# The first two up-steps of the last network moved into the second attention's block

## The chip, the cores and the metric

One core of a Trainium2 chip runs the whole program. The metric is the device time of one execution in microseconds (us). TensorE (PE) multiplies; VectorE (DVE), ScalarE (ACT) and GpSimd (Pool) work on tiles in SBUF and PSUM; SyncE (SP) issues most DMAs. Each engine works through its own instruction list in order and waits on semaphores for the others. TensorE's clock is one of two, 2.4 GHz (granted clock 1.00) or 1.2 GHz (0.50).

## The reference, cut to what matters

Two transformer layers over `x` of 2 x 1024 tokens with 256 features, all in float32. The change lies at the seam between the last two stages:

```python
x = x + _layernorm(_L0_attn_ref(_layernorm(x)))    # linear attention, 16 heads
x = x + _layernorm(_L0_ffn_ref(_layernorm(x)))     # 16 experts, top 2, and a shared network
x = x + _layernorm(_L1_attn_ref(_layernorm(x)))    # windows of 32 keys, 16 heads of 16
x = x + _layernorm(_L1_ffn_ref(_layernorm(x)))     # the last network

def _L1_ffn_ref(h_shard, w_gate_up, w_down):       # 256 -> 2 x 1024 -> 256
    gate, up = split(einsum('bsh,oh->bso', h_shard, w_gate_up))
    return einsum('bsi,hi->bsh', silu(gate) * up, w_down)
```

## The kernel before, in words

Matmuls that have to be exact are done in three passes: both operands are split into a rounded high part (ScalarE: `act_high`) and a remainder (VectorE: `dve_low`), and high x high, high x low and low x high are summed in PSUM.

**The second attention** (`window_attention`, one `nc.Block`) runs 16 jobs, `NJ = 16`: 2 batches (`NB = 8` jobs each) x 4 groups of windows x 2 groups of heads. A loop variable `i` counts the rounds in each engine's list, and every round holds pieces of several jobs, so that the job's stages overlap. TensorE in round `i`: scores of job `i` (L2841), transposes of the probabilities of job `i-2` (L2852), product with the values of job `i-3` (L2862), and, when `i-6` is odd, the output projection of job `i-6` (L2889), which waits for the eviction of the projection before. VectorE in round `i`: maximum and subtraction of job `i` (L2605, L2609), reciprocal of job `i-4` (L2634), transpose of job `i-5` (L2641), eviction of y for job `i-7` (L2650). ScalarE: the exponential of job `i` (L2740) and the copies of transposed probabilities (L2748) and raw products (L2755). Pool multiplies the products by the reciprocals (L2539) and does small work of the norms in a round's gap. Rounds 16 to 22 only finish jobs.

Scores are read from `q3`, which is filled by rearranging `q2` (`arrange`).

Around this stand two norms for the network that follows. `before` (an `AddNorm`) normalizes the attention's output y of a segment of 512 tokens, four tiles, and adds it to x: statistics on VectorE, `scale_and_shift` on Pool, `act_apply` on ScalarE, `add` (L1123). `turn` (a `TurnNorm`) normalizes the new x, transposes it on TensorE (`pe_turn`, L1157) and splits it into `xT_hi` (`act_high`) and `xT_lo` (`dve_low`). For segment 0, all of this is done in the attention's last rounds: `before.act_apply` in round 13, `before.add` and the turn's statistics in round 15, `turn.act_apply` in round 17, the transposes in round 21. In round 15, ScalarE also loads the table of the Silu.

When all engines have reached the block's end, Pool clears the semaphores of the stage, and its memset of `begun` (L1434) signals `ffn_ready`, for which every engine waits at the head of the next block.

**The last network** (`feed_forward`) handles 4 segments, each in `J = 8` steps of 128 inner features. An up-step (`pe_up`) is 12 matmuls of 128 x 512: gate and up, two halves of the features, three passes. In the first segment these are L1344, L1345 and L1348, with waits for the weights' parts. Then ScalarE does the Silu (`act_step`, L1299) and VectorE (`dve_step`) the product (L1314), its rounding (L1318) and its remainder (L1320). The down-step (`pe_down`, L1377, L1378, L1382) runs two steps behind. Up-steps alternate between two pairs of PSUM banks: up-step `n` waits until the product of step `n-2` is made. The weights come from DRAM unsplit, during the attention; they are split (L1245 and L1256 for up, L1249 and L1260 for down) in the first segment, two steps ahead of their use, steps 0 and 1 at the block's head. Also at the head, VectorE makes the statistics of `before` for segment 1, Pool scales, ScalarE applies after its first Silu (`before.act_apply(act, 1)`), and Pool adds (L1123). The turn of segment 1 gets its statistics after steps 2 and 3, is applied after step 4 and transposed on TensorE after up-step 5 and down-step 3.

## Time and profile before

| | us |
|---|---|
| median of 3 runs | 1158.51 |
| lowest and highest | 1154.85, 1162.67 |
| profiled execution | 1155.04 |
| its span | 1153.2 |
| mean granted clock of TensorE | 0.972 of full |

The times are those of an execution on the device. The profile belongs to one execution; its span runs from the first to the last instruction that it records. Starts in a timeline are counted from the span's start. A timeline's row gives start, duration, engine, line, operation, tile written and tiles read, and in square brackets how long the engine had been idle and which work released it; `x4` merges that many alike. Matmuls overlap, so the time that one takes from its queue is the distance to the next one's start.

The second attention's jobs fill the stretch up to about 1003 us, and the last network lies between about 1005 and 1147 us.

### The profile page before, as it was taken

The page shows a single profiled execution, that of the slowest core. Times are in us where ns is not written, and L with a number is a line of the kernel's source. Part 1 is how long each engine was busy: PE and PEld are TensorE (multiplying, and loading weights), DVE is VectorE, ACT ScalarE, POOL GpSimd, SP SyncE. Part 2 cuts the span into 40 slices and gives each one's busy share as a digit, 9 for nine tenths or more (in the row PEclk, how much of TensorE's full clock was granted, in tenths as well). Part 3 has the DMA queues.
Part 4 walks back from the last instruction along what each step waited for, and adds up shares of the span by engine and source line. Part 5 has one row for each costly group of instructions (what it writes and reads, how often), then busy time and mean ns, then how long its engine had stood idle before and what let it go on. Part 6 is the DMA issues. An engine that isn't in the chain of part 4 may idle for free. (4 is left out here: it accounts for less than half of the span.)

```text
span 1153.2 us, 20280 instructions
## 1 busy us (share of the span) xinstructions
PE 1114.8 (97%) x7188; PEld 960.1 (83%) x7188; DVE 743.3 (64%) x1582; ACT 525.1 (46%) x978; POOL 252.7 (22%) x290
## 2 busy tenths in 40 slices
PE   8999999999999999999999999899998889899997
PEld 7997988989989989988988888775555778788897
DVE  6665665665665665665665677755554767686556
ACT  5675344344344344344344354555552466644322
POOL 1112021021021021111111131323332556323211
PEclk9999999999999999999999999799998969999999
DMA  4001001001001001001000000853333324000001
GB/s 156 11 1 37 11 1 38 9 0 36 9 0 36 9 0 36 9 0 36 9 0 1 1 1 4 318 123 97 98 102 96 87 77 147 1 1 1 19 19 38
DMA packets 27979, 48.28 MB, mean 42 GB/s; under 512 B 4780, under 2 KB 18060, under 8 KB 26764
## 3 DMA queue, kind: packets, MB, share of 16 engines
q1 hardware_dynamic: 23980, 37.62, 10.2%
q0 software_dynamic: 3456, 9.44, 3.1%
q8 instruction: 37, 0.61, 0.2%
q10 hardware_dynamic: 480, 0.40, 0.1%
q14 instruction: 26, 0.21, 0.1%
HBM read 35.65 MB, written 9.44 MB: 39 GB/s over the span
## 5 line engine op out<-in xcount | busy, mean ns | idle before, releaser
L880 POOL TENSOR_TENSOR linear_out_row<-linear_out_row,lin_sq 128x512 f32<-128x512 f32 x62 | 89.9, 1450 | 538.3 <-ACT lin_sq L745 536.0
L43 PE MATMUL lin_bank<-keep_xT_hi,lin_w_hi 128*128 128x512 f32 x382 | 154.2, 404 | 0.0
L44 PE MATMUL lin_bank<-keep_xT_lo,lin_w_hi 128*128 128x512 f32 x382 | 151.1, 395 | 0.0
L45 PE MATMUL lin_bank<-keep_xT_hi,lin_w_lo 128*128 128x512 f32 x382 | 150.8, 395 | 0.0
L825 DVE TENSOR_TENSOR lin_st<-lin_bank,lin_mask 128x512 f32<-128x512 f32 x64 | 44.0, 691 | 160.9 <-PE lin_bank L622 160.9
L741 ACT ACTIVATE lin_o<-lin_bank 128x512 f32<-128x512 f32 x64 | 38.3, 599 | 187.7 <-PE lin_bank L653 187.7
L649 PE MATMUL lin_bank<-lin_st,lin_v 128*128 128x128 f32 x512 | 93.8, 275 | 0.0
L653 PE MATMUL lin_bank<-lin_qd,lin_state 128*128 128x128 f32 x448 | 87.2, 276 | 0.0
L45 PEld LDWEIGHTS lin_bank<-keep_xT_hi,lin_w_lo 128*128 128x128 f32 x382 | 71.8, 188 | 17.5
L44 PEld LDWEIGHTS lin_bank<-keep_xT_lo,lin_w_hi 128*128 128x128 f32 x382 | 72.0, 189 | 14.6
L43 PEld LDWEIGHTS lin_bank<-keep_xT_hi,lin_w_hi 128*128 128x128 f32 x382 | 72.0, 188 | 14.6
L649 PEld LDWEIGHTS lin_bank<-lin_st,lin_v 128*128 128x128 f32 x512 | 75.2, 192 | 0.0
L849 DVE SCALAR_TENSOR_TENSOR lin_state<-lin_state,lin_c_dec,lin_bank 128x128 f32<-128x128 f32 x192 | 65.3, 347 | 10.2 <-PE lin_bank L637 4.2
L43 PE MATMUL lin_bank<-lin_w_hi,keep_xT_hi 128*128 128x256 f32 x256 | 71.7, 280 | 0.0
L44 PE MATMUL lin_bank<-lin_w_lo,keep_xT_hi 128*128 128x256 f32 x256 | 71.5, 279 | 0.0
L45 PE MATMUL lin_bank<-lin_w_hi,keep_xT_lo 128*128 128x256 f32 x256 | 71.4, 279 | 0.0
L653 PEld LDWEIGHTS lin_bank<-lin_qd,lin_state 128*128 128x128 f32 x448 | 67.9, 192 | 0.0
L762 DVE TENSOR_TENSOR lin_g_lo<-lin_g,lin_g_hi 128x512 fp32r<-128x512 f32 x62 | 63.9, 1030 | 2.1
L710 ACT ACTIVATE lin_v<-lin_bank 128x512 f32<-128x512 f32 x64 | 38.0, 603 | 58.1 <-PE lin_bank L45 58.1
L622 PE MATMUL lin_bank<-lin_q,lin_k 128*128 128x128 f32 x512 | 63.9, 279 | 0.0
L792 DVE TENSOR_TENSOR linear_out_row<-linear_out_row,lin_bank 128x512 f32<-128x512 f32 x64 | 43.1, 685 | 30.3 <-PE lin_bank L45 30.3
L622 PEld LDWEIGHTS lin_bank<-lin_q,lin_k 128*128 128x128 f32 x512 | 61.2, 196 | 0.0
(417 smaller groups left out, 2843.2 us busy)
## 6 DMA issues: line engine op xcount, KB each, us to landing
lin_raw<-in_wp SPq DMA_DIRECT2D x7, 1024.0 KB, 4.7
experts_up_expert_up<-in_wgu SPq DMA_DIRECT2D x16, 352.0 KB, 7.3
sorted_y<-shared_loaded SPq DMA_DIRECT2D x40, 128.0 KB, 1.7
linear_out_row<-in_wdn SPq DMA_DIRECT2D x4, 704.0 KB
lin_raw_out<-in_wop SPq DMA_DIRECT2D x8, 256.0 KB, 2.6
tokens_x<-linear_out_row SPq DMA_DIRECT2D x4, 512.0 KB, 10.3
linear_out_row<-in_ffn_up SPq DMA_DIRECT2D x2, 1024.0 KB, 5.8
tail_q<-tail_qT SPq DMA_DIRECT2D x28, 64.0 KB, 2.0
```

What stands on the lines that cost most here:

```text
L43: nc.tensor.matmul(out, lh, rh, start=first, stop=False, skip_group_check=skip)
L44: nc.tensor.matmul(out, lh, rl, start=False, stop=False, skip_group_check=skip)
L45: return nc.tensor.matmul(out, ll, rh, start=False, stop=last, skip_group_check=skip)
L622: last = pe.matmul(bank[2 + a][:, cols], k[:, a, cols], q[:, a, cols], start=True, stop=True)
L649: last = pe.matmul(bank[a][:, cols], v[:, j, a, :], st[:, a, cols], start=True, stop=fresh)
L653: last = pe.matmul(bank[a][:, cols], state[:, a, j, :], qd[:, a, cols], start=False, stop=True)
L741: act.activation(o[:, a, :], bank[a][:], ACT.Copy).then_inc(o_sb, 1)
L762: dve.tensor_tensor(g_lo[:, a, :], g[:, a, :], g_hi[:, a, :].bitcast(F32), ALU.subtract).then_inc(g_sb, 1)
L792: dve.tensor_tensor(part, part, bank[4 + f][:], ALU.add).then_inc(acc_sb, 1)
L825: dve.tensor_tensor(C4(st[:, a, :]), C4(bank[2 + a][:]), mask[:, a:a + 1, :].broadcast_to([P, TPS, P]), ALU.mult).then_inc(st_sb, 1)
L849: dve.scalar_tensor_tensor(new, state[:, a, j, :], c_dec[:, a:a + 1], grown, ALU.mult, ALU.add).then_inc(state_sb, 1)
L880: pool.tensor_tensor(part, part, sq[:, a, :], ALU.add).then_inc(squares_sb, 1)
```

## The change

- **Two up-steps move.** Up-steps 0 and 1 of segment 0 are multiplied in the attention's block: up-step 0 in round 19 behind that round's output projection, after waits for the last subtraction, for the last copy of transposed probabilities and for both low parts of the turned segment; up-step 1 in round 21, behind the last output projection. The network's block begins with up-step 2. Its Silu, product and down-step of steps 0 and 1 stay there.
- **The up-weights of steps 0, 1 and 2** are rounded by ScalarE in rounds 12, 13 and 14 (`act_high_up`) and their remainder is taken by VectorE in rounds 15, 17 and 22 (`dve_low_up`). The parts of these weights lie where `q2` and `q3` were, so ScalarE waits for the last rearrangement and VectorE for the last scores. The down-weights are still split in the network's block. Splits of the steps from 3 on come behind the step three ahead of them.
- **The norms of segment 0 come sooner.** `before`'s scale and shift: Pool after job 6, not 7, with the shifts of x (`b.pool_shift_x`) after job 7, not 6; `act_apply` in round 11, not 13; `add` in round 13 and the turn's statistics in round 14, not both in round 15; the turn's scale after Pool's job 10, not 11; its apply in round 16, not 17; its transposes and high parts in round 18, its low parts in round 19, not 21.
- **Statistics of `before` for segment 1** move from the network's head into round 20.
- The PSUM banks, four semaphores, `q2` and `q3` now belong to an object (`Signals`) that both blocks share. `Fetched` holds it; the class that it was is now called `Loaded`. Norms without a turned part have four semaphores fewer.

The diff, cut to its core:

```diff
 
+class Signals:
+
+
+    NAMES = ("up_hi", "up_lo", "g_mm", "u_mm")
+
+    def __init__(self, nc, c):
+        self.made = {n: c.sem(f"ffn_{n}") for n in self.NAMES}
+        with ExitStack() as sooner:
+            self.q3 = sooner.enter_context(nc.sbuf_tensor("window_q3", [P, RR, WPAIRS, 4, WIN], F32))
+            self.q2 = sooner.enter_context(nc.sbuf_tensor("window_q2", [P, REP, WPAIRS * WIN], F32))
+        self.first = tuple(c.sb(n, [P, KT, 2 * sum(FFN)], F32R) for n in ("up_lo", "up_hi"))
+        self.bank = c.banks(8)
+
...
+
+    def __init__(self, scope, signals, others=True):
+        self.sb = scope.sb
+        self.sem = lambda name: signals.made[name] if name in signals.NAMES else scope.sem(name) if others else None
+
...
 
     def act_high(self, act, j):
 
-        w = self.widths[j]
+        self.act_high_up(act, j)
+        if not self.whole_down:
+            self.act_high_down(act, j)
+
+    def act_high_up(self, act, j):
         act.wait_ge(self.up_in, KT * DMA)
         for cols in self.columns(j):
             act.activation(self.w_hi[:, :, cols], self.raw[:, :, cols], ACT.Copy).then_inc(self.up_hi, 1)
-        if self.whole_down:
-            return
+
+    def act_high_down(self, act, j):
+        w = self.widths[j]
         act.wait_ge(self.down_in, self.J * DMA)
         act.activation(self.d_hi[0:w, j, :], self.raw_d[0:w, j, :], ACT.Copy).then_inc(self.down_hi, 1)
 
...
@@ -1405,8 +1447,10 @@
 
 
     with Scope(nc, "ffn") as c:
-        bank = c.banks(8)
-        net = Swiglu(nc, c, keep, y, bank, FFN, weights=SwigluWeights(c, FFN, fetched))
+        signals = fetched.signals
+        bank = signals.bank
+        room = Room(c, signals)
+        net = Swiglu(nc, room, keep, y, bank, FFN, weights=SwigluWeights(room, FFN, fetched, signals.first))
...
@@ -1450,16 +1494,15 @@
             def _(dve):
                 chain = Chain(dve, own)
                 dve.wait_ge(keep.ffn_ready, 1)
-                net.dve_low(dve, 0)
-                for half in range(2):
-                    before.statistics(dve, chain, 1, half)
-                net.dve_low(dve, 1)
+                net.dve_low_down(dve, 0)
                 for g in range(SEGS):
                     late = LATE if g == 0 else 0
                     for j in range(J):
-                        if g == 0 and j + 2 < J:
-                            net.dve_low(dve, j + 2)
                         net.dve_step(dve, chain, g, j)
+                        if g == 0 and j < 2:
+                            net.dve_low_down(dve, j + 1)
+                        if g == 0 and j + 3 < J:
+                            net.dve_low(dve, j + 3)
                         if 0 <= j - late < 2 and g + 1 < SEGS:
                             dve.wait_ge(before.added, g + 2)
                             turn.statistics(dve, chain, g + 1, j - late)
@@ -1486,14 +1529,15 @@
             @block.scalar
             def _(act):
                 act.wait_ge(keep.ffn_ready, 1)
-                net.act_high(act, 0)
-                net.act_high(act, 1)
+                net.act_high_down(act, 0)
                 for g in range(SEGS):
                     late = LATE if g == 0 else 0
                     for j in range(J):
-                        if g == 0 and j + 2 < J:
-                            net.act_high(act, j + 2)
                         net.act_step(act, g, j)
+                        if g == 0 and j < 2:
+                            net.act_high_down(act, j + 1)
+                        if g == 0 and j + 3 < J:
+                            net.act_high(act, j + 3)
                         if g == j == 0:
                             before.act_apply(act, 1)
                         if g + 1 < SEGS:
@@ -1523,7 +1567,8 @@
                 for g in range(SEGS):
                     pe.wait_ge(turn.low, KT * (g + 1))
                     for j in range(J):
-                        net.pe_up(pe, g, j)
+                        if g or j >= 2:
+                            net.pe_up(pe, g, j)
 
                         if j >= 2 or g:
                             n = g * J + j - 2
...
@@ -2403,13 +2449,14 @@
 
     with Scope(nc, "tail") as c:
         sb = c.sb
-        sorted_y = keep.sorted_y
-
-        q3 = sb("q3", [P, RR, WPAIRS, 4, WIN])
+        sorted_y, signals = keep.sorted_y, fetched.signals
+
+        q3, q2 = signals.q3, signals.q2
         sb("rest_of_split", [P, 256])
-        bank = c.banks(8)
+        bank = signals.bank
         net = Swiglu(nc, c, keep, y, bank, SHARED, SHARED_EARLY, keep.shared)
         net.split_before = True
+        ffn = Swiglu(nc, Room(c, signals, False), keep, y, bank, FFN, 0, SwigluWeights(Room(c, signals, False), FFN, fetched, signals.first, True), True)
...
@@ -2545,12 +2591,12 @@
                     if n == 5:
                         a.pool_shift_x(pool)
                     if n == 6:
+                        before.affine.scale_and_shift(pool, chain, 0)
+                    if n == 7:
                         b.pool_shift_x(pool)
                     if n == 8:
                         c1.add(pool)
-                    if n == 7:
-                        before.affine.scale_and_shift(pool, chain, 0)
-                    if n == 11:
+                    if n == 10:
                         turn.affine.scale_and_shift(pool, chain, 0)
 
             @block.vector
@@ -2607,9 +2653,10 @@
                         if i >= 2:
                             dve.wait_ge(prob_sb, i - 1)
                         dve.tensor_tensor(by_window(less[x]), scores, spread_w(most[x][:]), ALU.subtract).then_inc(less_sb, 1)
-                    if i == NJ - 1:
+                    if i == NJ - 3:
                         dve.wait_ge(a.shifted, a.n)
                         before.add(dve, 0)
+                    if i == NJ - 2:
                         dve.wait_ge(before.added, 1)
                         for half in range(2):
                             turn.statistics(dve, chain, 0, half)
@@ -2652,8 +2699,18 @@
                         if t < 2:
                             dve.wait_ge(y_sb, t + 1)
                             before.statistics(dve, chain, 0, t)
-                    if i == NJ + 5:
+                    if i == NJ - 1:
+                        dve.wait_ge(s_mm, NJ)
+                        ffn.dve_low_up(dve, 0)
+                    if i == NJ + 1:
+                        ffn.dve_low_up(dve, 1)
+                    if i == NJ + 3:
                         turn.dve_low(dve, 0)
+                    if i == NJ + 4:
+                        for half in range(2):
+                            before.statistics(dve, chain, 1, half)
+                    if i == NJ + 6:
+                        ffn.dve_low_up(dve, 2)
 
             @block.scalar
             def _(act):
@@ -2761,13 +2818,20 @@
                     if i == NB - 1:
                         arrange(RR + 1, 0)
                         arrange(RR + 1, 1)
-                    if i == NB + 5:
+                    if i == NB + 3:
                         before.act_apply(act, 0)
+                    if i == NB + 4:
+                        for n in range(BATCH * RR):
+                            act.wait_ge(q3_sb[n], 2)
+                        ffn.act_high_up(act, 0)
+                    if i in (NB + 5, NB + 6):
+                        ffn.act_high_up(act, i - NB - 4)
                     if i == NJ - 1:
                         act.activation(table[:], power[:, 0:1], ACT.Silu)
-                    if i == NJ + 1:
+                    if i == NJ:
                         turn.act_apply(act, 0)
-                turn.act_high(act, 0)
+                    if i == NJ + 2:
+                        turn.act_high(act, 0)
 
             @block.tensor
             def _(pe):
@@ -2873,7 +2937,7 @@
                         project_q(1, i - 4)
                     if i == 6:
                         turn_v(1)
-                    if i == NJ + 5:
+                    if i == NJ + 2:
                         turn.pe_turn(pe, 0)
                     if 6 <= i < NJ + 6 and JOBS[i - 6][1] == RR - 1:
                         n = i - 6
@@ -2889,6 +2953,13 @@
                                 last = pe.matmul(bank[5][:, a * HID:(a + 1) * HID], oP[:, b, rr, tile * P:(tile + 1) * P], wo[:, rr, :],
                                                  start=rr == 0, stop=rr == RR - 1)
                         last.then_inc(y_mm, 1)
+                    if i == NJ + 3:
+                        pe.wait_ge(less_sb, NJ)
+                        pe.wait_ge(pT_sb, NJ)
+                        pe.wait_ge(turn.low, KT)
+                        ffn.pe_up(pe, 0, 0)
+                    if i == NJ + 5:
+                        ffn.pe_up(pe, 0, 1)
```

## Rows read from the trace of the kernel before

**Rows 1.** The page, busy time, share of the span and instructions of each engine.
```profile
PE 1114.8 (97%) x7188; PEld 960.1 (83%) x7188; DVE 743.3 (64%) x1582; ACT 525.1 (46%) x978; POOL 252.7 (22%) x290
```

**Rows 2.** Windows: us, busy us and (x) instructions per engine, mean granted clock, DMA share, GB/s.
```profile
984.00:990.00 6.00, 6.00 (x45) 5.19 (x44) 4.21 (x8) 4.23 (x10) 2.15 (x3) 1.00 0.00 0
1006.00:1013.00 7.00, 7.00 (x26) 5.57 (x25) 6.11 (x19) 4.68 (x14) 1.99 (x5) 0.76 0.00 0
```

**Rows 3.** Timeline of TensorE, end of the attention: start, us, engine, line [wait <-releaser].
```profile
989.57 1.94 PE L2889 MATMUL tail_bank<-window_wo,tail_oP 128*128 128x256 f32 x8
994.26 1.08 PE L2862 MATMUL tail_bank<-tail_v,tail_pT 128*128 128x68 f32 x8 [1.02 <-ACT tail_raw_o L2755]
1001.22 1.97 PE L2889 MATMUL tail_bank<-window_wo,tail_oP 128*128 128x256 f32 x8 [0.33 <-DVE keep_y L2650]
```

**Rows 4.** Timeline of TensorE, first segment of the last network.
```profile
1005.57 0.47 PE L1344 MATMUL ffn_bank<-keep_xT_hi,ffn_w_hi 128*128 128x512 f32 x1 [2.39 <-ACT ffn_w_hi L1245]
1012.72 0.39 PE L1344 MATMUL ffn_bank<-keep_xT_hi,ffn_w_hi 128*128 128x512 f32 x1
1015.47 0.28 PE L1377 MATMUL ffn_bank<-ffn_d_hi,ffn_h_hi 128*128 128x256 f32 x1
1030.63 1.09 PE L1157 MATMUL ffn_bank<-keep_ident,window_turn_z 128*128 128x128 f32 x8 [0.83 <-ACT window_turn_z L1129]
```

**Rows 5.** Timeline of VectorE, both blocks.
```profile
985.66 0.69 DVE L2605 TENSOR_REDUCE tail_most<-tail_bank 128x16 f32<-128x512 f32 x1 [2.00 <-PE tail_bank L2841]
987.46 0.65 DVE L2650 TENSOR_TENSOR keep_y<-tail_bank,window_bo 128x512 f32<-128x512 f32 x1
989.51 1.22 DVE L1123 TENSOR_TENSOR keep_x<-keep_x,window_before_z 128x1024 f32<-128x1024 f32 x1
992.63 0.22 DVE L2634 RECIPROCAL tail_inv<-tail_raw_o 128x16 f32<-128x16 f32 x1
1003.29 0.69 DVE L2650 TENSOR_TENSOR keep_y<-tail_bank,window_bo 128x512 f32<-128x512 f32 x1 [0.89 <-PE tail_bank L2889]
1017.90 0.75 DVE L1256 TENSOR_TENSOR ffn_w_lo<-linear_out_row,ffn_w_hi 128x256 fp32r<-128x256 f32 x2
1018.91 0.68 DVE L1314 TENSOR_TENSOR ffn_h<-ffn_silu,ffn_bank 128x512 f32<-128x512 f32 x1
1020.76 0.74 DVE L1007 BATCH_NORM_STATS2 window_turn_stats<-keep_x 128x6 f32<-128x256 f32 x2
```

**Rows 6.** Timeline of Pool, both blocks.
```profile
975.57 4.53 POOL L2315 TENSOR_SCALAR keep_x<-keep_x,tail_used_shift_y 128x256 f32<-128x256 f32 x5
983.14 1.81 POOL L2293 TENSOR_TENSOR keep_x<-keep_x,tail_spare 128x768 f32<-128x768 f32 x1
1004.88 0.10 POOL L1434 MEMSET ffn_begun<- 128x1 f32 x1 [4.86 <-POOLq L2487]
1012.83 2.42 POOL L1123 TENSOR_TENSOR keep_x<-keep_x,window_before_z 128x1024 f32<-128x1024 f32 x1 [2.19 <-ACT window_before_z L1129]
```

**Rows 7.** Timeline of ScalarE, both blocks.
```profile
991.05 1.28 ACT L2767 ACT_TABLE_LOAD   x1
1005.01 0.72 ACT L1245 ACTIVATE ffn_w_hi<-linear_out_row 128x256 fp32r<-128x256 f32 x2 [3.44 <-POOL ffn_begun L1434]
1007.78 0.57 ACT L1299 ACTIVATE ffn_silu<-ffn_bank 128x512 f32<-128x512 f32 x1
1010.67 2.08 ACT L1129 ACTIVATE window_before_z<-keep_y,window_before_shift,window_before_scale 128x256 f32<-128x256 f32 x4 [2.32 <-POOL window_before_shift L1035]
```

**Rows 8.** The page, DMA issues: KB each, us from issue to landing.
```profile
linear_out_row<-in_ffn_up SPq DMA_DIRECT2D x2, 1024.0 KB, 5.8
```

**Rows 9.** Line 1256: duration in ns, least/median/most, first and last start.
```profile
L1256 DVE TENSOR_TENSOR ffn_w_lo<-linear_out_row,ffn_w_hi x16: 391/417/2437, 1005.5 to 1031.3; 128x256 fp32r<-128x256 f32 x16
```

**Rows 10.** TensorE after a long pause: timeline and window.
```profile
923.47 1.88 PE L2810 MATMUL tail_bank<-keep_ident,tail_oP 32*128 32x32 f32 x16 [4.90 <-ACT tail_oP L2680]
920.00:947.00 27.00, 19.52 (x94) 16.90 (x95) 16.56 (x44) 17.09 (x32) 15.40 (x18) 0.56 0.34 92
```

More of the change, by code:

```diff
@@ L1170, in dve_low @@
                               ALU.subtract).then_inc(self.low, 1)
-class Fetched:
+class Loaded:
     def __init__(self, c, widths, up, down):
@@ L1212, with __init__ @@
 class Swiglu:
-    def __init__(self, nc, c, keep, y, banks, widths, start=0, weights=None):
+    def __init__(self, nc, c, keep, y, banks, widths, start=0, weights=None, only_up=False):
         self.start = start
@@ L1229, in __init__ @@
         self.up_in, self.down_in, self.up_hi, self.down_hi, self.up_lo, self.down_lo = w.up_in, w.down_in, w.up_hi, w.down_hi, w.up_lo, w.down_lo
-        self.silu, self.h = c.sb("silu", [P, 2, SEG]), c.sb("h", [P, 2, SEG])
-        if not self.whole_down:
+        if not only_up:
+            self.silu, self.h = c.sb("silu", [P, 2, SEG]), c.sb("h", [P, 2, SEG])
+        if not self.whole_down and not only_up:
             self.d_lo, self.d_hi = w.d_lo, w.d_hi
@@ L1251, in dve_low, with dve_low_up @@
     def dve_low(self, dve, j):
-        w = self.widths[j]
+        self.dve_low_up(dve, j)
+        if not self.whole_down:
+            self.dve_low_down(dve, j)
+    def dve_low_up(self, dve, j):
         for i, cols in enumerate(self.columns(j)):
@@ L2245, in __init__ @@
         self.known, self.affine_ready, self.z_ready = ({k: c.sem(f"{tag}_{n}_{k}") for k in kinds} for n in ("known", "affine", "z"))
-        self.added, self.turned, self.high, self.low = (c.sem(f"{tag}_{n}") for n in ("added", "turned", "high", "low"))
+        self.added = c.sem(f"{tag}_added")
         self.z_dve = c.sem(f"{tag}_z_dve") if by_dve else None
-        self.shifted = c.sem(f"{tag}_shifted")
+        if turned:
+            self.turned, self.high, self.low, self.shifted = (c.sem(f"{tag}_{n}") for n in ("turned", "high", "low", "shifted"))
         self.z = z
```

18 lines of the change are left out of this document (11 added, 7 removed).

## The prediction

> **What bounds the kernel now.** I read the engine totals first: TensorE is busy 97% of the span, so time comes off only where it stands still or runs slowly [rows 1]. The windows then say what limits the two stages that the change joins. While scores are still being made, the tensor engine fills the window completely, 6.00 of 6 us, with VectorE at 4.21: the attention's second half is bound by matmuls [rows 2]. The start of the last network is continuous too, but its mean clock is 0.76 [rows 2]. That is 7 x (1 - 0.76) / 0.5 = 3.4 us at 1.2 GHz instead of 2.4, after which the clock is back; lost: half of it, some 1.65 us. The fall follows a pause of the engine.
>
> Where is that pause? The timeline of TensorE shows 1.02 us of waiting before the fourteenth value product, 0.33 us before the last output projection, which ends at 1001.22 + 1.97 = 1003.19 us, and 2.39 us at the block boundary [rows 3, 4]. In the network, one up-step lasts 1015.47 - 1012.72 = 2.75 us at full clock; the first two took 1012.72 - 1005.57 = 7.15 us, and 7.15 - 5.50 = 1.65 is again the clock. The next wait is 0.83 us at the turn of segment 1, which starts at 1030.63 [rows 4]. So the stretch holds 1.35 + 2.39 + 1.65 + 0.83 = 6.2 us that are not work at full speed. The change can have that at the most.
>
> **The attention's tail.** Two up-steps move in front of the block's end: 2 x 2.75 = 5.50 us of matmuls. They don't lie beside other work of TensorE, they lengthen its queue there by as much. What can be won are its waits, so I laid out the four queues with the durations of the rows, job by job.
>
> Job 13: VectorE now has 2.00 us of waiting ahead of job 14's maximum [rows 5]. The add of segment 0 (1.22 us) moves into it, ends near 983.6, and the wait is still about 1.4 us long: free, if nothing holds the add up. For it ScalarE's norm comes two jobs sooner, and Pool's scale and shift goes ahead of the 4.53 us of shifts that started at 975.57 [rows 6]; both have the room, and the shifts end 2 us later, at 982.6.
>
> Job 14: add and statistics took 992.63 - 989.51 = 3.12 us, 1.25 of it for the add, so the statistics take 1.87 [rows 5]. They stand ahead of the transpose and of the eviction of y. Scores 14 still come at 985.66, so the difference ends at 987.1, the statistics at 988.9, transpose and reciprocal at 989.3, the eviction at 990.0 instead of 987.46 + 0.65 = 988.1. The ninth output projection, which started at 989.57 [rows 3], waits for that eviction: 0.5 us. The subtraction of job 15 ends at 991.4, not 989.6. ScalarE's last exponential, its copies and the table load of 1.28 us [rows 7] follow, 1.8 us later than before, less what ScalarE waited: value product 13 waits some 0.5 us for its predecessor's copy, and product 14 0.7 us. Then the transposes come right after product 15, near 998.7, and projection 13. The new wait of TensorE, for the low part of the turned segment, comes at 1001.5; ScalarE's and VectorE's copies (1.08 and 1.29 us, one after the other) end near 1002.2: 0.7 us. Behind that wait stands the last projection, and for that the last eviction. Sum of waits: 0.5 + 0.5 + 0.7 + 0.7 = 2.4 against 1.35. The second up-step therefore ends at 1003.19 + 5.50 + 1.05 = 1009.7.
>
> The weight splits cost VectorE 0.75 us each [rows 5], in jobs 15, 17 and 22, and ScalarE 0.72 us each [rows 7] at jobs 12 to 14, where it waits for VectorE. The last split and the last eviction, 1.4 us together, are covered by the second up-step's 2.75. Statistics of segment 1, 1.9 us, fall between evictions, covered by the first. The weights are long in SBUF: issued before 964, they land in about 6 us [rows 8]. The loads are the same and keep their place on SP's queue; no DMA is added. Fewer semaphores and the other place of two buffers: nothing.
>
> **The boundary.** Before, the block ended with VectorE's eviction, at 1003.29 + 0.69 = 1003.98, and Pool's memset that starts the network came 0.90 us later [rows 5, 6]. Now TensorE is last, so the memset is at 1010.6. But the third up-step needs the product of the first in the same PSUM bank. Released by the memset come 0.13 us to ScalarE, 0.31 for one rounding of down-weights (from the start of one activation to the next), 0.57 for the Silu, 0.04, VectorE's product 0.69 and 0.08. Up-step 3 starts at 1009.7 + 0.90 + 1.82 = 1012.4 where it was at 1012.72 [rows 4, 7]: -0.3 us. The pause of TensorE is 2.7 us, longer than the 2.39 that it replaces. **The clock** thus falls again: between 0 (if it does not) and 1.65 us, and I take 1.65, since the nearest pause is shorter and paid it.
>
> **The first segment.** From up-step 3 to the turn took 1029.80 - 1012.72 = 17.08 us; now TensorE is there at 1012.4 + 17.08 + 1.65 = 1031.2. Is z there? VectorE begins its first product at 1011.7. A step is 1020.76 - 1018.91 = 1.85, a split of up and down 1.01, its down part about 0.3, half of the statistics 0.94 [rows 5]. It waits for the second Silu, which stands behind ScalarE's 2.08 us norm [rows 7] (end of Silu: 1015.4), and its cast behind Pool's 2.42 us add, until 1017.3. Then 1.07 for cast and rest, 0.33 + 1.01 + 1.85 + 1.01 + 0.94 + 1.85 + 1.01 + 0.94: the statistics are done at 1027.4. Pool 2.1 to 2.8 and ScalarE 2.08 follow: 1031.6 to 1032.3, middle 1032.0 against 1030.63. The stall shrinks but stays, and the sum is +1.4 us.
>
> One step in this rests on row and rule. The split that met Pool's add took 2437 ns instead of a median 417 [rows 6, 9]. The Trainium skill (SBUF — State Buffer, Who interferes with whom) says that a VectorE instruction with two SBUF inputs and a GpSimd instruction that reads SBUF use a shared port, and that the second waits for the whole of the first; the trace agrees with the 2437 ns.
>
> **The sum.** The profiled execution took 1155.04 us around its span of 1153.2, so 1156.4 by this; it lies 3.5 below the median of the three runs. From that median, 1158.51, I get 1159.9.
>
> **Rivals.** *The tail is filled.* My waits rest on chains of four engines laid out by hand; my layout of the old tail was 0.5 us off. If the two up-steps swallow all but 0.3 us of waits, the second ends at 1007.6, and everything behind it starts 2.1 us sooner; VectorE's chain then lets the turn start at 1029.9 in the middle, and if its backlog is gone as well and the clock stays, at 1027.4. That is -0.7 to -3.2, middle -2: 1156.5. For it: removing 3.1 us from VectorE between the last difference and the last value products. Against it: statistics in job 14 delay the same difference. Chance 0.22.
>
> *Slower by the port.* The moved add has two SBUF inputs. At its old place, 989.51, Pool was idle; at 982.4 Pool is at its shifts, then at the product of job 8 and at a 1.8 us add. If VectorE loses, it waits until 985.0, 2.6 us, and 1.4 of that is covered: the point from which it decides. The first two weight splits can meet Pool's 0.62 us products as well. Price: 1.2 + 2 x 0.6 = 2.4 on top of 1.4, +3.8: 1162.3. The 2437 ns [rows 9] speak for a price of up to 2.0 for one collision, the slack of VectorE against it. Chance 0.14. By the rule of the Trainium skill named above, the loser is whichever issues second, so it would go this way only if Pool is first.
>
> *The clock stays down.* After a pause of 4.90 us, and with waits between its matmuls behind it, TensorE had a mean clock of 0.56 over the 27 us from 920 to 947 [rows 10]: 27 x 0.44 / 0.5 = 24 us at 1.2 GHz. If the new pause of 2.7 us and a late product did that here, 24 us at half speed would cost 12 in place of 1.65: +11.8, so 1170.3. Against it: it needs waits inside the first steps, and VectorE has its products ready there. Chance 0.02.
>
> *The change does nothing at all*, because matmuls are neither added nor removed: this is what my forecast nearly says.
>
> **Chances.** Forecast (0 to +2.7) 0.62. A measurement of this kernel can tell about 1% (11.6 us) from no change; only the last rival and an unforeseen mishap pass it: slower 0.02, faster 0.01, same 0.97. The runs shown reach from 3.7 below to 4.2 above their median. So the range goes from 1158.5 - 2 - 2.5 = 1154 to 1158.5 + 2.7 + 3.8 = 1165, which holds the forecast, most of the filled tail and of the port.
>
> **What would show it.** Right: two up-steps among the last projections, and a wait of some 0.7 us ahead of the first; a pause near 2.7 us at the boundary that ends with VectorE's product; again some 3.4 us at 0.5 behind it; the turn's start between 1031.5 and 1032.5. Wrong: a boundary pause below 2 us, a clock that holds, an add of over 1.3 us in job 13, or a turn without a wait.

## The result, and the profile after

The changed kernel took 1163.15 us in the median of 20 executions (1158.46 to 1166.64); the kernel before took 1158.42 (1154.85 to 1162.67) beside it. The ratio is 1.0037, 95% interval 1.0025 to 1.0049. By the ratio that is 4.3 us more (2.9 to 5.7), under 1%; forecast were 1.4. The median lies inside the forecast's range of 1154 to 1165, but that range was wide because single executions scatter: the loss itself lies above the 0 to 2.7 us that the prediction gave for it.

The engine totals of the changed kernel, to be held against [rows 1]:

```profile
span 1161.0 us, 20285 instructions
...
PE 1118.2 (96%) x7188; PEld 961.4 (83%) x7188; DVE 743.4 (64%) x1582; ACT 525.7 (45%) x978; POOL 254.4 (22%) x290
```

TensorE's busy time grew too, which says little, since a matmul at 1.2 GHz is busy for longer. The timeline says more. Here is TensorE in the attention's tail, the counterpart of [rows 3] (start and duration in us, engine, line, tiles; in brackets the idle time ahead and its releaser). The first row is the start of job 15's scores, from which I count below:

```profile
992.37 0.48 PE L2905 MATMUL window_bank<-linear_out_row,window_q 64*128 64x128 f32 x2
...
995.49 0.67 PE L2953 MATMUL window_bank<-window_wo,tail_oP 128*128 128x256 f32 x2 [0.36 <-DVE keep_y L2697]
...
998.25 0.52 PE L2926 MATMUL window_bank<-tail_v,tail_pT 128*128 128x68 f32 x3 [0.36 <-ACT tail_raw_o L2812]
...
1000.54 0.52 PE L2926 MATMUL window_bank<-tail_v,tail_pT 128*128 128x68 f32 x3 [0.77 <-ACT tail_raw_o L2812]
...
1005.06 0.60 PE L2953 MATMUL window_bank<-window_wo,tail_oP 128*128 128x256 f32 x2
...
1007.00 0.47 PE L1386 MATMUL window_bank<-keep_xT_hi,window_up_hi 128*128 128x512 f32 x1
...
1009.84 0.59 PE L2953 MATMUL window_bank<-window_wo,tail_oP 128*128 128x256 f32 x2
```

Three waits, 0.36 + 0.36 + 0.77 us. The first up-step (1007.00) begins right behind projection 13, without a wait. Now the boundary and the first segment, [rows 4] of before. The second row is the fourth up-step, the third row the turn of segment 1:

```profile
1017.35 0.76 PE L1386 MATMUL window_bank<-keep_xT_hi,window_up_hi 128*128 128x512 f32 x1 [2.86 <-ACT window_up_hi L1281]
...
1023.88 0.50 PE L1386 MATMUL window_bank<-keep_xT_hi,window_up_hi 128*128 128x512 f32 x1 [0.63 <-DVE ffn_h L1356]
...
1038.67 0.55 PE L1157 MATMUL window_bank<-keep_ident,window_turn_z 128*128 128x128 f32 x3 [1.94 <-ACT window_turn_z L1129]
```

Two stretches of the same engine, answering to [rows 2] (length, busy us and count, mean granted clock, DMA share, GB/s): behind the pause the clock is low again.

```profile
1007.00:1014.00 7.00, 7.00 (x31) 1.00 0.00 0
1018.00:1022.00 4.00, 4.00 (x15) 0.69 0.00 0
```

The turn came 1030.63 - 986.98 = 43.65 us after job 15's scores before [rows 4], and comes 1038.67 - 992.37 = 46.30 after them now: **2.65 us of the loss lie here.** What made it late is on VectorE. These are its rows, answering to [rows 5]: first product, the remainders of the down-weights of steps 1 and 3 (counted from 0), second product, end of the turn's statistics:

```profile
1016.41 0.69 DVE L1356 TENSOR_TENSOR ffn_h<-ffn_silu,window_bank 128x512 f32<-128x512 f32 x1
...
1018.21 0.42 DVE L1302 TENSOR_TENSOR ffn_d_lo<-linear_out_row,ffn_d_hi 128x256 fp32r<-128x256 f32 x1
...
1021.29 1.94 DVE L1302 TENSOR_TENSOR ffn_d_lo<-linear_out_row,ffn_d_hi 128x256 fp32r<-128x256 f32 x1 [1.99 <-ACT ffn_d_hi L1286]
...
1023.15 0.67 DVE L1356 TENSOR_TENSOR ffn_h<-ffn_silu,window_bank 128x512 f32<-128x512 f32 x1
...
1033.69 0.25 DVE L1012 BATCH_NORM_AGGREGATE window_turn_mean_var<-window_turn_stats 128x2 f32<-128x6 f32 x2
```

And ScalarE's and Pool's for the same time, answering to [rows 6, 7]: ScalarE's roundings of the down-weights of steps 1 and 3, the first part of its norm, the second Silu, the rounding of step 2; then Pool's add:

```profile
1016.28 0.41 ACT L1286 ACTIVATE ffn_d_hi<-linear_out_row 128x256 fp32r<-128x256 f32 x1
...
1017.20 0.40 ACT L1286 ACTIVATE ffn_d_hi<-linear_out_row 128x256 fp32r<-128x256 f32 x1
...
1018.38 0.60 ACT L1129 ACTIVATE window_before_z<-keep_y,window_before_shift,window_before_scale 128x256 f32<-128x256 f32 x1 [0.78 <-POOL window_before_shift L1035]
...
1020.37 0.57 ACT L1341 ACTIVATE ffn_silu<-window_bank 128x512 f32<-128x512 f32 x1
...
1020.85 0.41 ACT L1286 ACTIVATE ffn_d_hi<-linear_out_row 128x256 fp32r<-128x256 f32 x1
...
1020.54 2.40 POOL L1123 TENSOR_TENSOR keep_x<-keep_x,window_before_z 128x1024 f32<-128x1024 f32 x1 [2.19 <-ACT window_before_z L1129]
```

VectorE stood still for 1.99 us ahead of 1021.29, and the profile names ScalarE's `ffn_d_hi` as the releaser. The remainder that waited is that of **step 3**, and ScalarE had rounded the down-weights of step 3 long before, at 1017.20. But all these roundings raise one counter, `down_hi`, and VectorE waits for step 3 with "at least 4". ScalarE's new order is 0, 1, 3, then the norm (2.08 us), the second Silu, and only then 2, at 1020.85. The counter reaches 4 with the rounding of step 2: the wait is for the wrong data. In addition the delayed instruction now falls into Pool's add of 2.40 us and takes 1.94 us in place of the 0.42 of its like (1018.21). So the second product starts at 1023.15.

The profiled span is 1161.0 - 1153.2 = 7.8 us longer, and not all of it is the change's. From the first up-step of the shared network to job 0's scores: 42.2 us before, 47.5 after. But the kernel before, profiled a second time, had 46.5 there, and the changed one 42.9. So this part varies by 4.3 and 4.6 us between two executions of one program.

### The profile page after: what moved, and what is told of

Its sections match the earlier page's. It is cut to its first block and busy times, and to the rows that moved or that the text cites. A ratio compares the mean times of both kernels' runs of the same rounds, so it can differ in the third digit from the quotient of the medians.

```text
span 1161.0 us, 20285 instructions
## 1 busy us (share of the span) xinstructions
PE 1118.2 (96%) x7188; PEld 961.4 (83%) x7188; DVE 743.4 (64%) x1582; ACT 525.7 (45%) x978; POOL 254.4 (22%) x290
```

## The experiments

Twelve runs, each timed in five rounds; the ratio is to the kernel before, timed beside it. "Job 7 to 11" and "job 15 to turn" are distances on TensorE between starts of scores and, for the last, the start of the turn's transposes for segment 1; "turn to turn" goes on from there to the transposes for segment 2. "Low" is the time at 1.2 GHz in that distance, from its mean granted clock, and good to about 0.4 us.

| kernel | ratio, 95% interval | job 7 to 11 (low) | job 15 to turn (low) | turn to turn (low) |
|---|---|---|---|---|
| before | | 15.44 (3.4) | 43.65 (3.5) | 26.32 (0) |
| before_again | 0.9998, 0.9980 to 1.0017 | 15.44 (3.4) | 43.64 (3.5) | 26.32 (0) |
| placed | 1.0002, 0.9987 to 1.0016 | 15.30 (0) | 43.60 (0) | 26.33 (0) |
| norms | 1.0012, 0.9998 to 1.0027 | 15.44 (3.4) | 44.87 (3.6) | 26.08 (0) |
| changed | 1.0037, 1.0025 to 1.0049 | 17.07 (6.8) | 46.30 (3.7) | 26.08 (0) |
| again | 1.0030, 1.0018 to 1.0041 | 18.33 (7.0) | 46.23 (0) | 27.67 (3.4) |
| third | 1.0020, 1.0003 to 1.0038 | 18.33 (7.0) | 46.26 (0) | 27.68 (3.4) |
| in_order | 1.0013, 1.0002 to 1.0024 | 18.34 (7.0) | 44.88 (0) | 26.33 (0) |
| in_order_again | 1.0006, 0.9989 to 1.0022 | 18.32 (7.0) | 44.89 (0) | 26.32 (0) |
| one_step | 1.0008, 0.9998 to 1.0018 | 15.30 (0) | 44.95 (0) | 26.32 (0) |
| both | 1.0011, 0.9997 to 1.0024 | 15.29 (0) | 43.60 (0) | 27.91 (3.4) |
| early_two | 0.9999, 0.9985 to 1.0013 | 19.95 (10.4) | 43.61 (3.5) | 26.27 (0) |
| early_one | 0.9997, 0.9984 to 1.0010 | 15.30 (0) | 43.50 (3.5) | 26.27 (0) |
| early_one_again | 0.9983, 0.9968 to 0.9997 | 15.30 (0) | 41.79 (0) | 26.27 (0) |

From job 11 to job 15 it is 13.95 to 13.97 us in all of them, and from the second turn to the end of the span 96.3.

### Is it the orders, or where things lie? (placed, again)

placed has the shared object, its buffers and semaphores, but every engine's order of before; in outline, against the kernel before:

```diff
 class Signals: ...            # as in the change
-    bank = c.banks(8)
+    bank = signals.bank       # and q2, q3, up_lo, up_hi from it
```

> The shared object, the other places of two buffers and the shared PSUM banks alone; every list of instructions in the order of before. Theory 1 (the loss is made at the seam between the blocks, by the order of the work): as before, ratio 1.000, and the stretch from job 12's scores to the turn of segment 1 is 53.1 us long as before. Rival (the placement itself costs what the seam does not explain, some 2 us of the 4.7): ratio 1.002, and the head of the attention's block, from the first up-step of the shared network to the first transposes of values, is longer than the 40.4 us of before.

again is the changed kernel once more.

> The changed kernel once more, for a second profile. Its first profile has 5.4 us more than before ahead of job 12's scores, 5.9 of them in one gap near 895, in which VectorE and ScalarE both stand still, and 2.7 us more at the seam. Theory 1: the gap is chance and does not come again at this place, the 2.7 us do; ratio 1.002 to 1.005. Rival (the gap belongs to the change): it is there again.

placed costs nothing: 1.0002, and 43.60. Again lost 3.5 us (2.1 to 4.7), and 46.23 between job 15 and the turn. The loss comes from the orders. The column up to the turn shows something else: in placed and in again the clock **did not fall** behind the boundary, and the distance to the turn stayed the same as with the fall. Here is again:

```profile
1013.99 0.47 PE L1386 MATMUL window_bank<-keep_xT_hi,window_up_hi 128*128 128x512 f32 x1 [2.90 <-ACT window_up_hi L1281]
...
1020.45 0.50 PE L1386 MATMUL window_bank<-keep_xT_hi,window_up_hi 128*128 128x512 f32 x1 [2.02 <-DVE ffn_h L1356]
...
1035.22 0.55 PE L1157 MATMUL window_bank<-keep_ident,window_turn_z 128*128 128x128 f32 x3 [1.93 <-ACT window_turn_z L1129]
```

Clock full, so TensorE is ready for the fourth up-step 1.4 us sooner, and the fourth waits for VectorE's product 2.02 us where it waited 0.63. The low clock in this place is hidden by VectorE's chain. In placed the fourth up-step waits 1.27 us in the same way, and the distance is that of before.

But in again the clock fell a little later, behind the turn's wait of 1.93 us. Again's TensorE from 1036 to 1040 us, and its next turn:

```profile
1036.00:1040.00 4.00, 4.00 (x13) 0.57 0.00 0
...
1062.89 1.03 PE L1157 MATMUL window_bank<-keep_ident,window_turn_z 128*128 128x128 f32 x8
```

There nothing hides it: from turn to turn it takes 27.67 us, in the first profile of the same program, where the clock held, 26.08. third and both show the same fall at the same place (27.68 and 27.91), the eleven other profiles none. The changed kernel paid for no low clock between job 15 and the second turn in one profile, and 1.6 us in two; the kernel before in neither of its two.

### The counter (in_order)

The changed kernel, with this:

```diff
-                        if g == 0 and j < 2:
-                            net.dve_low_down(dve, j + 1)
+                        if g == 0 and j == 0:
+                            net.dve_low_down(dve, 1)
+                            net.dve_low_down(dve, 2)
```

and the same for ScalarE's `act_high_down`, so that the counter rises in the order of the waits.

> The changed kernel with the down-weights of steps 1 and 2 both rounded and subtracted ahead of those of step 3, so that the counter of rounded down-weights rises in the order in which VectorE waits for it. Theory 1 (the remainder of down-weights 3 waits for the rounding of down-weights 2, which stands behind ScalarE's norm and Silu, is then caught by Pool's add, and puts VectorE 2 us behind): the wait of 2.0 us ahead of that remainder and its 1.9 us are gone, no wait of TensorE before up-step 3, the turn's statistics 1 to 1.5 us sooner, the turn's wait 1.9 becomes 1.2 to 1.5, and 1.0 to 1.3 us are won against the changed kernel. Rival (Pool's add holds up VectorE anyway, at the cast): under 0.4 us won.

> Both up-steps moved and the down-weights' parts counted in the order of the waits, a second time. Program theory: over 6 us of low clock in jobs 8 to 10 again. Chance theory: as likely as not under 5. From job 15 to the turn 44.9; ratio 1.0005 to 1.0020.

In the first of the two, VectorE's first product, step 3's remainder, second product, its cast, end of statistics; then Pool's add and TensorE's turn:

```profile
1017.35 0.69 DVE L1356 TENSOR_TENSOR ffn_h<-ffn_silu,window_bank 128x512 f32<-128x512 f32 x1
...
1020.49 0.41 DVE L1302 TENSOR_TENSOR ffn_d_lo<-linear_out_row,ffn_d_hi 128x256 fp32r<-128x256 f32 x1
...
1021.91 0.69 DVE L1356 TENSOR_TENSOR ffn_h<-ffn_silu,window_bank 128x512 f32<-128x512 f32 x1 [1.01 <-ACT ffn_silu L1341]
...
1022.63 1.53 DVE L1360 CAST ffn_h_hi<-ffn_h 128x512 fp32r<-128x512 f32 x1
...
1033.24 0.25 DVE L1012 BATCH_NORM_AGGREGATE window_turn_mean_var<-window_turn_stats 128x2 f32<-128x6 f32 x2
...
1021.48 2.41 POOL L1123 TENSOR_TENSOR keep_x<-keep_x,window_before_z 128x1024 f32<-128x1024 f32 x1 [2.19 <-ACT window_before_z L1129]
...
1038.21 0.55 PE L1157 MATMUL window_bank<-keep_ident,window_turn_z 128*128 128x128 f32 x3 [2.62 <-ACT window_turn_z L1129]
```

The remainder takes 0.41 us and stands ahead of Pool's add; the second product follows the first by 4.56 us, not 6.74. Pool's add now catches the cast behind that product, as the prediction had it: 1.53 us, where the next cast takes 0.43. No wait ahead of the fourth up-step. 44.88 and 44.89 us to the turn: 1.4 less than the changed kernel, and its ratio fell with it, to 1.0013 and 1.0006. That the counter costs 1.4 us is shown. The turn still waits 2.62, for the norm that begins when the statistics end; expected were 1.2 to 1.5. z comes 1.4 us sooner than in the changed kernel, but TensorE is there 2.1 us sooner.

### One up-step instead of two (one_step, both)

```diff
-                        if g or j >= 2:
+                        if g or j >= 1:
                             net.pe_up(pe, g, j)
...
-                    if i == NJ + 5:
-                        ffn.pe_up(pe, 0, 1)
```

> The changed kernel with up-step 1 back at the head of the network's block; only up-step 0 is multiplied in the attention's. Theory 1 (what two steps in front cost is a boundary with nothing for TensorE to do until Silu and product of step 0 are made): the pause at the boundary falls from 2.9 us to 1.8 to 2.1, and 0.8 to 1.0 us are won up to up-step 2; as the turn then waits for VectorE's chain, which starts when the block does, 0 to 1 us of it reaches the end. Rival (the second step in front is what fills the tail): lost 1 us or more.

both adds the order of in_order.

> One up-step moved, and the down-weights in counter order. Each of the two won 1.3 to 1.4 us up to the turn of segment 1, measured from job 15's scores (44.9 instead of 46.3; before 43.65). Theory 1 (they stand on the same chain of VectorE behind each other): together 43.4 to 43.8, so no longer slower than before, ratio 1.000. Rival (they buy the same wait): 44.5 or more.

```profile
1010.70 0.50 PE L1386 MATMUL window_bank<-keep_xT_hi,window_up_hi 128*128 128x512 f32 x1 [2.47 <-POOL ffn_begun L1478]
...
1032.49 0.55 PE L1157 MATMUL window_bank<-keep_ident,window_turn_z 128*128 128x128 f32 x3 [1.87 <-ACT window_turn_z L1129]
```

Neither of the two needs the first product ahead of its second up-step, so the pause was expected shorter; it is 2.47 us, for the block now ends with VectorE's last eviction and one split behind it, which my 1.8 to 2.1 left out. one_step won 1.35 us up to the turn, both another 1.35, and ends at 43.60: as before the change, with one up-step in the tail. For one_step 0 to 1 us had been expected. The turn's wait (1.87) is now the whole of what stands still in the first segment. Its times (1.0011) don't show the last 1.35. In its profile the clock fell behind the turn and cost 27.91 - 26.32 = 1.6 us there, so that up to the second turn it is again 1.5 us longer than before.

### The norms by themselves (norms)

The changed kernel, with splits, up-steps and the statistics of segment 1 back at the network's head; only segment 0's norms stay two jobs sooner.

```diff
-                net.dve_low_down(dve, 0)
+                net.dve_low(dve, 0)
+                for half in range(2):
+                    before.statistics(dve, chain, 1, half)
+                net.dve_low(dve, 1)
```

> Of the change only the norms of segment 0 that come sooner, and the shared object; both up-steps, all splits of weights and the statistics of segment 1 stand in the network's block as before. Theory 1: the sooner norms alone cost or win little: TensorE waits 0.36 us in round 15 for the eviction behind the moved statistics, 1.1 us in the products behind it as before, and is not held at the turn; the time from job 15's scores to the turn of segment 1 stays within 0.5 of the 43.6 us of before. Rival (VectorE's add meeting Pool is what costs): 1 to 2 us longer.

```profile
992.64 0.67 PE L2936 MATMUL window_bank<-window_wo,tail_oP 128*128 128x256 f32 x2 [0.36 <-DVE keep_y L2696]
...
995.40 0.52 PE L2909 MATMUL window_bank<-tail_v,tail_pT 128*128 128x68 f32 x3 [0.36 <-ACT tail_raw_o L2801]
...
997.69 0.52 PE L2909 MATMUL window_bank<-tail_v,tail_pT 128*128 128x68 f32 x3 [0.77 <-ACT tail_raw_o L2801]
...
1005.04 0.67 PE L2936 MATMUL window_bank<-window_wo,tail_oP 128*128 128x256 f32 x2 [0.94 <-DVE keep_y L2696]
```

The sooner norms cost 44.87 - 43.65 = 1.2 us: the same three waits as in the changed kernel, and 0.94 ahead of the last projection. Expected had been less than 0.5 us, so this was a miss. The rival had the size, 1 to 2 us, but not the cause: the add in job 13 met Pool here too, and VectorE still waited 0.92 us for the scores behind it. What holds TensorE up are evictions and copies that now stand behind the turn's statistics and its low parts. The sooner norms are a price paid for a z that is ready when an up-step can use it, and win nothing by themselves. 44.87 is also what in_order reaches (44.88), so the moved up-steps with their splits neither won nor lost anything up to the turn once the counter is in order; the 2.65 us of the changed kernel are 1.2 for the norms and 1.4 for the counter.

### The norm of segment 1 taken along (early_two, early_one)

If VectorE, Pool and ScalarE are late at the turn, the whole first norm of segment 1 can be done in the tail. Beside what in_order has:

```diff
                     if i == NJ + 1:
-                        ffn.dve_low_up(dve, 1)
+                        for half in range(2):
+                            before.statistics(dve, chain, 1, half)
...
+                    if n == 13:
+                        before.affine.scale_and_shift(pool, chain, 1)
...
+                before.act_apply(act, 1)
...
+                before.add(pool, 1)
```

and the scale, the apply and the add go out of the network's head. The statistics of segment 1 stood in round 20 and change places with the remainder of the up-weights of step 1. early_one has one up-step in the tail, early_two both.

> The same with both up-steps in the attention's block. Theory 1 (the second step in front buys nothing: the boundary keeps a pause of 2.9 us and the clock falls behind it): the turn's wait is gone too, and it takes 43.3 to 43.9 us, 0.6 to 0.9 more than with one step. Rival (two steps are better as soon as the norm is out of the way): equal to one step or shorter.

> As the kernel with one up-step and the counter order, and the whole norm before the network of segment 1 (statistics in round 17, Pool's scale after job 13, ScalarE's apply behind the turned segment's high parts, Pool's add behind job 15) in the attention's block, where ScalarE and Pool otherwise stand still. Theory 1 (VectorE's chain behind ScalarE's norm and Pool's add is what delays the turn of segment 1): the turn no longer waits, VectorE has no wait ahead of product 1, and job 15's scores to the turn take 42.6 to 43.2 us, 0.5 to 1.0 less than before; ratio 0.999. Rival (the norm lengthens the attention's last rounds by what it wins): 43.6 or more.

> One up-step moved, parts in order, and the whole norm ahead of the turn of segment 1 in the attention's block, a second time. In its first profiled execution the clock fell for 3.5 us behind the boundary, and as nothing waited at the turn this cost 1.65 us in full: 43.50. If the clock holds behind the boundary this time: 41.8 to 42.0. If it falls: 43.5. Program theory of the clock: no low clock in jobs 8 to 10; chance theory: as likely as not some. Ratio 0.9985 to 1.0005.

The turn waits no more, in all three. In the first run of early_one this brought 0.1 us over both, less than expected, and the first window (TensorE busy us and count, granted clock, DMA share, GB/s) shows why; in the second run, to which all rows behind it belong, the one difference is the clock:

```profile
1012.00:1018.00 6.00, 5.98 (x19) 0.72 0.00 0
```
```profile
1011.38 0.51 PE L1386 MATMUL window_bank<-keep_xT_hi,window_up_hi 128*128 128x512 f32 x1 [2.47 <-POOL ffn_begun L1478]
...
1031.01 0.49 PE L1157 MATMUL window_bank<-keep_ident,window_turn_z 128*128 128x128 f32 x3
```
```profile
1012.00:1016.00 4.00, 4.00 (x19) 1.00 0.00 0
1016.00:1031.00 15.00, 15.00 (x90) 1.00 0.01 2
```

6 x 0.28 / 0.5 = 3.4 us at 1.2 GHz in the first, none in the second, and 43.50 - 41.79 = 1.71 us between them. **Where the turn waits for VectorE's chain the low clock is free; where nothing waits it costs its full 1.7.** The same holds behind the turn (again, third, both). The second run is 0.9983, faster than the kernel before by 0.3 to 3.7 us. The first was 0.9997. Both weighted by their intervals give 0.9991, 0.9981 to 1.0001: the best kernel of the study, and not surely better than the one before.

### A second look at the clock (before_again, third)

All kernels with both up-steps in the tail had spent longer on jobs 7 to 11 in their profile, ahead of everything that was moved there. So the kernel before and the changed one were profiled once more.

> The kernel before, once more, for a second profiled execution. Its first showed a low clock for some 3.5 us in the attention's jobs 7 to 9 and 3.4 us behind the boundary. Chance theory (the falls differ from execution to execution of one program): the fall in jobs 7 to 10 has another length here, between 0 and 7 us, and the mean clock of the executions is again near 0.976. Program theory (each program has its own falls): again 3 to 4 us there. Either way from job 15's scores to the turn of segment 1: 43.6, and a ratio of 1.000 within 0.0015.

> The changed kernel a third time. Its two profiled executions, and those of the two other kernels with both up-steps moved, all showed 6.5 to 10 us of low clock in jobs 8 to 10, which costs 3.3 to 5; the three with one step or none had none there, the kernel before 3.5 and the one with sooner norms 4. Program theory: again over 6 us here, and this is the part of the measured loss that the 2.65 us between job 15 and the turn do not hold. Chance theory: as likely as not under 5 us. From job 15's scores to the turn 46.2 to 46.3 by both; ratio 1.0023 to 1.0040.

third and then before_again, TensorE in the same two stretches of 8 us:

```profile
960.00:968.00 8.00, 6.53 (x52) 1.00 0.41 85
968.00:976.00 8.00, 8.00 (x37) 0.57 0.97 374
```
```profile
960.00:968.00 8.00, 8.00 (x47) 0.79 0.37 83
968.00:976.00 8.00, 8.00 (x58) 1.00 0.96 370
```

and TensorE's pause ahead of it in third, at the scores of job 8:

```profile
966.40 0.57 PE L2905 MATMUL window_bank<-linear_out_row,window_q 64*128 64x128 f32 x3 [1.47 <-issue]
```

The chance theory fell for the profiled executions: 17.07 to 19.95 us in six of six with two moved up-steps, 15.29 to 15.44 in eight of eight others. The pause of 1.47 us ahead of job 8 is in placed, one_step, both and early_one as well, and there the clock holds. In before, norms and the changed kernel's first profile the clock falls sooner, and the pause is gone: the 3.4 us at 1.2 GHz of before make this stretch only 0.14 us longer (15.44 against 15.30), since they fill the pause; the 7.0 behind the pause make it 3.0 longer. And the timed executions don't bear it out: in_order and both differ by 3.05 us in jobs 7 to 11, but by 0.0002 in their ratios (from job 15 to the second turn they differ by 0.3 us alone), and early_two and the first early_one by 4.65 us and 0.0002. The profiled executions of early_two, in_order and third took 4.7, 4.0 and 3.3 us more than their kernels' medians, so that a fall in these alone would fit; those of again and in_order_again took 0.6 and 0.2 more and that of the changed kernel 0.3 less, with such a fall too, and that doesn't fit. The mean granted clock over all executions of the changed kernel is 0.9744 (44 of them), over those of the kernel before in three rounds beside it 0.9755 (105 of them); 0.0011 of 1160 us is 1.3 us, give or take 1.1.

## Why the prediction was right in direction and too small

**The attention's tail.** Forecast waits: 0.5, 0.5, 0.7 and 0.7. Measured: 0.36, 0.36, 0.77 and none ahead of the first up-step. The layout of the four queues held, but for z, which was there in time. The two up-steps took 2.8 us each. End of the second, from job 15's scores: 22.1 us, forecast 22.7. (The shifts on Pool ended where the prediction had them, 4.4 us ahead of job 15's scores; that is 2.5 us later than in [rows 6], not the 2 us that stand beside it.)

**The boundary.** Forecast a pause of 2.7 ended by ScalarE and VectorE, measured 2.86. The profile's releaser is `window_up_hi`, but by the code the parts that this up-step needs were made in the attention; what it had to wait for last was VectorE's product of 1016.41. Third up-step 0.76 us sooner than the same one of before, forecast 0.3.

**The clock.** It fell (about 3.5 us at 1.2 GHz) as forecast, but in again and third it did not fall there, and their distance to the turn is the same within 0.07 us. So my 1.65 was no term of the sum at this place. The text had this right without saying so: it took the later of TensorE's 1031.2 and z's 1032.0. That a clock which holds at the boundary can fall behind the turn, where it costs 1.6, the prediction did not have.

**The first segment: this step failed**, and with it the size. I wrote the VectorE chain from its own durations, from ScalarE's norm and Pool's add, and had its statistics done 40.4 us after job 15's scores. They were done 41.6 after them. I had listed ScalarE's instructions, but not asked which of them VectorE's counter would count. The change makes both engines split the down-weights of step 3 ahead of those of step 2 only in one place of their lists, and puts a norm between. With the counter in order (in_order) the statistics end at 1033.49 - 993.33 = 40.2 and the turn starts at 44.88, where my forecast was 1032.0 - 986.98 = 45.02. The counter's 1.4 us are what the sum lacked: 1.4 + 1.4, less 0.15, is the 2.65 measured.

**The sum.** The three measurements of the changed kernel, weighted by their intervals, give 1.0031 (1.0024 to 1.0038): 3.6 us, 2.8 to 4.4. The 2.65 lie just under its lower edge. From job 15's scores to the second turn, the three profiles of the changed kernel take 72.38, 73.90 and 73.94 us against 69.97 and 69.96 before and 69.94 in placed: 2.4, 3.9 and 4.0 more, 3.4 in the mean. So the fall behind the turn has the size of what the 2.65 lack, and the mean clock of the executions has it too. Three profiles don't show how often it comes, and why the clock falls at one of the two places and not at the other no run shows; nor is it shown that the lower clock in jobs 7 to 11 costs the timed executions nothing. That the median lies within the range is in part luck: the range reaches 3.8 us beyond the 2.7. The port's rival came nearest with its 3.8 us more, and that by chance, as its collision cost nothing.

**The rivals.** *The tail is filled* did not happen: the waits in the tail grew from 1.35 to 1.49. *Slower by the port* was right in its mechanism and wrong in its price. Here is the moved add, with Pool's work beside it:

```profile
987.92 1.75 DVE L1123 TENSOR_TENSOR keep_x<-keep_x,window_before_z 128x1024 f32<-128x1024 f32 x1
...
991.05 0.69 DVE L2651 TENSOR_REDUCE tail_most<-window_bank 128x16 f32<-128x512 f32 x1 [0.91 <-PE window_bank L2905]
...
987.97 0.61 POOL L2585 TENSOR_TENSOR tail_o<-tail_raw_o,tail_inv 128x256 f32<-128x256 f32 x1
...
988.55 2.79 POOL L2339 TENSOR_TENSOR keep_x<-keep_x,tail_spare 128x768 f32<-128x768 f32 x1
```

The add took 1.75 us, not 1.22, and Pool's sum 2.79, not 1.81. VectorE still waited 0.91 for job 14's scores, so this cost nothing; the point from which it decides was not reached. The rule cited in the prediction (the Trainium skill, SBUF — State Buffer, Who interferes with whom) gives these durations to within 0.15 us: the add ends 1.22 us after Pool's product has ended (987.97 + 0.61 + 1.22 = 989.80, measured 989.67), and Pool's sum 1.81 after the add (989.67 + 1.81 = 991.48, measured 991.34). The collision that did cost was the one with Pool's add in the first segment, and it is there in every order that has this add in the network: 2.44 us in place of 0.42 for a split before [rows 9], 1.94 for the remainder in the changed kernel, 1.53 in place of 0.43 for the cast in in_order. The counter only chose which instruction it caught. *The clock stays down* did not happen in any of 14 profiles.

## What to carry to other kernels

When instructions change places in two engines' lists, check every counting semaphore between them: a wait for "n of them" is a wait for the n-th in the producer's order, and the profile names it as an idle time released by a line whose data the waiting instruction doesn't read. The crossing can be a hazard as well: by the code, the remainder of step 2 waits for 3 roundings, which step 3's satisfies, and only its place behind step 3's remainder in VectorE's list keeps its data safe. Before you price a slower clock or a stall, ask which engine's chain is later at the next meeting point; here 1.65 us of low clock were worth nothing as long as the turn waited for VectorE, and all of it once it didn't, or when the clock fell just behind the turn. So follow two kernels up to a point behind the last wait that differs. And compare two profiles by distances between fixed points of the program, since two executions of one program differed by 4 to 5 us ahead of the place in question.

## What was unexpected of the hardware

- The clock's fall at a given pause is no property of the pause: at 2.34 us it held in placed and fell in norms, at 2.47 it held in both and fell in early_one, at 2.86 it held in in_order and fell in the changed kernel. A fall lasted about 3.5 us there. In three of the eight profiles in which it held, it fell behind the next wait (1.85 to 1.93 us, at the turn) instead.
- In the attention's jobs 7 to 11 one program mostly shows the same fall again (15.44 and 15.44 us; 18.34 and 18.32; 18.33 twice and 17.07 once), and a program with the same orders up to there another one (both: 15.29). Behind the boundary the same programs differ from execution to execution.
- A VectorE instruction with two inputs in SBUF that met Pool's add waited for its end: 1.94 us instead of 0.42, and in early_one 2.96 for a pair of weight remainders that takes 0.75 elsewhere. A cast with one input was held up too: 1.53 us instead of 0.43 in in_order.
